# A shared expert's second product from 64 rows per half, and both second-pair gates ahead of the third layer's products, in a vision tower kernel

## The chip, the cores and the metric

The kernel runs on one core of a Trainium2 chip. The metric is the device time of one execution in microseconds (us), the median over a few executions; one further execution is recorded by the profiler.

## What is computed

Four images of 3 x 224 x 224 become 784 tokens of 64 numbers each (patches of 8 x 8, layer norm, two linear layers). Then come four residual blocks: a gated linear attention that here reduces to a product, a first layer of experts, a softmax attention with 8 heads, and a second layer of experts. The change is in the first layer of experts:

```python
# x: normalised tokens, 64 features; E = 4 experts, 2 chosen per token
h = relu(x @ sW1 + sb1)                 # shared path: 64 -> 64
h = relu(h @ sW2 + sb2)                 # 64 -> 128, the product that changes
shared = h @ sW3 + sb3                  # 128 -> 64
h = relu(x @ eW1[e] + eb1[e])           # each expert: 64 -> 128
h = relu(h @ eW2[e] + eb2[e])           # 128 -> 64
all_out[e] = h @ eW3[e] + eb3[e]        # 64 -> 64
out = shared + sum over the two best experts of topw * all_out[e]
```

## The kernel before

Features lie on the 128 partitions and tokens along them. The tokens of an image are split in two halves of 392; half 0 has its 64 features on partitions 0 to 63, half 1 on partitions 64 to 127. So one tile `[128, 392]` holds an image. Every engine has a program of its own, written out in order, and they meet through semaphores.

The first expert layer loops over the four images `b`. For each, TensorE issues in this order (the loop stands in the listing below):

- the experts' second layer (key "l2", pairs of experts p = 0, 1 and halves h = 0, 1): two products of 128 rows by 64 columns each, one for output partitions 0 to 63 and one for 64 to 127;
- the shared path's second product (key "s2", one for each half), line 853. Its weight `sw2` is `[128, 2, 128]`. The host fills rows 0 to 63 of part 0 and rows 64 to 127 of part 1 with `sW2` and leaves zeros in the other rows, so each product runs over all 128 rows of `s1`, though only 64 of them count;
- `gate_rows`: four transposes that turn the image's gate values into rows (key "wT");
- `first_layer(b + 1)`: the shared path's first product (key "s1"), and 8 outputs "l1" (4 experts, 2 halves) of two products each, in the format fp32r, for the next image;
- the third layer of image b: broadcasts of gates 0 and 1 (`broadcast_gate`, which spreads a gate's row over 128 partitions of bank 5 or 6), two products with `eb3r` (the output biases), two with `sw3` (the shared path), and then for m = 0 to 3 the broadcast of gate m + 2 if there is one, a wait until the m-th gated tile is ready, and the product `ew3` with it. Even m write partitions 0 to 63 of bank 7, odd m partitions 64 to 127.

A product of plain fp32 is two matmul instructions in the trace, one in fp32r is one. In the trace `s1` and `s2` are named `s`, `h1` and `h2` are `h`, the gate rows are `wT`, and all weights of the first table are `wa`. Nearly all products stand under line 679, the helper `mm`.

The outputs of the keys l2, s2, wT, s1 and l1 go round a ring of four PSUM banks (`bank_of`): an output may start once ScalarE has emptied the one four places before it. ScalarE (ACT) empties them one by one and in order with `hidden` (line 513), with bias and relu. VectorE (DVE) multiplies each `h2` tile by its broadcast gate in place (`times_gate`, line 1359): it waits for `wbc_full` and raises `wbc_done`. `broadcast_gate` for gate n waits until multiplication n - 2 is done, as the two banks 5 and 6 alternate. After the third layer VectorE adds bank 7 to `H` (line 1365), and ScalarE may write the next image's `h2`. After image 3 come the attention's layer norm (products with `H`, squares, variance, reciprocal root) and the attention.

Of the kernel before, what the change touches and what calls it, by code (L numbers as in the profile page):

```python
# [19 lines left out]
D = 64  # L20
# [14 lines left out]
E0, E1 = 4, 8  # L35
# [67 lines left out]
def build(nc, x, table_a, table_b, out):  # L103
    ctx = ExitStack()
    with ctx:
        def sem(name):
            return ctx.enter_context(nc.semaphore(name))

        def sb(stack, name, shape, dt=F32):
            return stack.enter_context(nc.sbuf_tensor(name, shape, dt))  # L110
# [19 lines left out]
        sel0r = sb(reg1, "sel0r", [96, E0 // 2, 2, 128], F32R)  # L130
# [22 lines left out]
        s1 = sb(reg1, "s1", [128, HALF])  # L153
        s2 = sb(reg1, "s2", [128, 2, HALF])
        gate0 = Gate(lambda n, shape, dt=F32: sb(reg1, n, shape, dt), E0)
        wT0 = sb(reg1, "wT0", [96, HALF], F32R)
# [43 lines left out]
        def bank(n, w=HALF):  # L200
            return P[:, n, 0:w]

        def A(name, rows=128):
            lo, hi = COLS_A[name]
            return wa[0:rows, lo:hi]
# [40 lines left out]
        hid_full, hid_done = sem("hid_full"), sem("hid_done")  # L246
# [430 lines left out]
        def _(pe):  # L677
            def mm(dst, lhsT, rhs, start=True, stop=True, **more):
                return nc.tensor.matmul(dst, lhsT, rhs, start=start, stop=stop, **more)  # L679
# [122 lines left out]
            def bank_of(key, first):  # L802

                k = HID[key]
                n, size = k % 4, 4
                if k - size >= first:
                    pe.wait_ge(hid_done, k - size + 1)
                elif k < size:
                    pe.wait_ge(h_ready, B)
                return n  # L810

            def gate_rows(n, wsp, b, full):
                for ct in range(NGT):
                    last = nc.tensor.transpose(P[0:96, n, ct * GT:(ct + 1) * GT], wsp[:, ct * B + b, :].bitcast(F32),  # L814
                                               Bt("ident", GT)[:, 0:GT])
                last.then_inc(full, 1)
# [3 lines left out]
            sw2 = A("sw2").rearrange("p (h n) -> p h n", h=2)  # L820

            def first_layer(b):
                mm(bank(bank_of(("s1", b), 0)), A("sw1"), xhat[:, b, :]).then_inc(hid_full, 1)
                pe.wait_ge(split0, 2 * b + 2)
                if b == 0:
                    pe.wait_ge(w0_split, 1)
                for e in range(E0):
                    for h in range(2):
                        n = bank_of(("l1", b, e, h), 0)
                        for part in range(2):  # L830
                            last = mm(bank(n), ew1r[:, part, e, :], xs0[:, b, h * HALF:(h + 1) * HALF], part == 0, part == 1)
                        last.then_inc(hid_full, 1)

            def broadcast_gate(sel, rows, n):

                if n >= 2:
                    pe.wait_ge(wbc_done, n - 1)
                mm(bank(WBC_BANKS[n % 2]), sel, rows).then_inc(wbc_full, 1)
# [4 lines left out]
            for b in range(B):  # L843
                for p in range(E0 // 2):
                    pe.wait_ge(hid_done, HID["l1", b, 2 * p + 1, 1] + 1)
                    for h in range(2):
                        n = bank_of(("l2", b, p, h), 0)
                        for e in range(2):
                            last = mm(P[e * D:(e + 1) * D, n, 0:HALF], ew2[:, 2 * p + e, :], h1[:, 2 * p + e, h, :])
                        last.then_inc(hid_full, 1)  # L850
                pe.wait_ge(hid_done, HID["s1", b] + 1)
                for h in range(2):
                    mm(bank(bank_of(("s2", b, h), 0)), sw2[:, h, :], s1[:, :]).then_inc(hid_full, 1)
                if b == 0:
                    pe.wait_ge(gates_ready, 1)
                gate_rows(bank_of(("wT", b), 0), gate0.wsp, b, hid_full)
                if b + 1 < B:
                    first_layer(b + 1)
                pe.wait_ge(hid_done, HID["wT", b] + 1)
                if b == 0:  # L860
                    pe.wait_ge(sel0_ready, 1)
                for m in range(2):
                    broadcast_gate(sel0r[:, 0, m, :], wT0[:, :], E0 * b + m)
                if b >= 1:
                    pe.wait_ge(h_ready, B + b)
                for part in range(2):
                    mm(bank(7), eb3r[:, part, :], wT0[:, :], part == 0, False, skip_group_check=True)
                for h in range(2):
                    mm(P[h * D:(h + 1) * D, 7, 0:HALF], A("sw3"), s2[:, h, :], False, False, skip_group_check=True)
                for m in range(E0):  # L870
                    if m + 2 < E0:
                        broadcast_gate(sel0r[:, 1, m, :], wT0[:, :], E0 * b + m + 2)
                    pe.wait_ge(wbc_done, E0 * b + m + 1)
                    h = m % 2
                    last = mm(P[h * D:(h + 1) * D, 7, 0:HALF], ew3[:, m // 2, :], h2[:, m // 2, h, :], False,
                              m // 2 == E0 // 2 - 1, skip_group_check=True)
                last.then_inc(moe_full, 1)
# [217 lines left out]
            for b in range(B):  # L1095
# [7 lines left out]
                for p in range(PAIRS):  # L1103
                    m = PAIRS * b + p
# [528 lines left out]
```

## Time and profile before

| what | value |
|---|---|
| median of three executions | 628.32 us |
| the three | 628.19, 628.32, 632.11 us |
| the profiled execution, its own time | 634.78 us |
| its span, first to last instruction | 633.0 us |
| mean granted TensorE clock | 0.979 of full |
| TensorE busy | 574.7 us, 91% |
| VectorE, ScalarE, GpSimd busy | 383.1, 335.3, 73.8 us |
| share of the chain that ended last | PE 87%, DVE 5%, ACT 4%, DMA 2% |

The profile is one execution. Its span is 1.8 us shorter than its own time, which has also what lies before the first and behind the last instruction. A matmul's time is its latency; consecutive ones overlap, so their cost is read from the distance of their starts.

### The profile page before, as it was taken

The numbers are of one execution on the slowest core, as the hardware profiler recorded it, in microseconds if no ns is written. First come the engines' busy times: TensorE is split into PE (matmuls) and PEld (weight loads), VectorE is DVE, ScalarE is ACT, GpSimd is POOL, SyncE is SP. The second block draws the span as 40 slices with busy tenths as digits, with TensorE's granted clock in tenths as the row PEclk, the third lists the DMA queues.
The fourth block names the chain that finished last, engine by engine and source line by source line (L and its number), as shares of the span: only waits on it lengthen the run. The fifth ranks groups of instructions, "written<-read, shape, count | busy, mean of one in ns | idle before, by whom it ended". The sixth has DMA issues, their size and how long they took to land.

```text
span 633.0 us, 10237 instructions
## 1 busy us (share of the span) xinstructions
PE 574.7 (91%) x3082; PEld 341.8 (54%) x3082; DVE 383.1 (61%) x896; ACT 335.3 (53%) x735; POOL 73.8 (12%) x88
## 2 busy tenths in 40 slices
PE   0597798999798999999999999999999999997992
PEld 0363344654446766757667566675666756452441
DVE  3847458123487776767767677676776765145561
ACT  0455857754654655646556465464664646525411
POOL 0000000000299001010010100101001010102000
PEclk9999899999897999999999999999999999997997
DMA  7500000000363233232332422323223220000024
GB/s 164 220 0 1 1 0 2 0 1 0 71 151 90 58 80 87 67 98 60 83 83 57 102 63 79 87 56 98 68 76 90 56 73 1 1 1 1 1 50 103
DMA packets 21986, 37.65 MB, mean 59 GB/s; under 512 B 5560, under 2 KB 15224, under 8 KB 21704
## 3 DMA queue, kind: packets, MB, share of 16 engines
q1 hardware_dynamic: 21816, 37.12, 22.9%
q10 hardware_dynamic: 144, 0.20, 0.2%
q8 instruction: 14, 0.23, 0.2%
q14 instruction: 12, 0.10, 0.0%
HBM read 6.07 MB, written 2.41 MB: 13 GB/s over the span
## 4 chain that ended last, share of the span: by engine, by line
PE 87%; DVE 5%; ACT 4%; DMA 2%; issue 1%; SPq 0%; DVEq 0%; ACTq 0%
PE P L679 83%; DMA X<-x 2%; PE P L695 2%; ACT L481 1%; DVE xhat L1204 1%; PE P L940 1%; ACT PT L590 1%; ACT g L622 1%; DVE xs L1273 1%; PE P L1079 0%; DVE mx L1378 0%; DVE gate_s L1261 0%; PE P L814 0%; DVE bst L1141 0%; PE P L910 0%
## 5 line engine op out<-in xcount | busy, mean ns | idle before, releaser
L1378 DVE TENSOR_REDUCE mx<-P 112x1 f32<-112x392 f32 x448 | 219.4, 558 | 97.2 <-PE P L679 92.5
L590 ACT ACTIVATE PT<-P 112x392 f32<-112x392 f32 x448 | 188.4, 494 | 27.3 <-PE P L679 26.1
L679 PE MATMUL P<-Ks,Qs 96*112 96x392 f32 x448 | 167.9, 379 | 1.0 <-DVE mx L1378 0.9
L679 PE MATMUL P<-Qs,Ks 98*112 98x392 f32 x448 | 155.5, 351 | 0.8 <-ACT PT L590 0.7
L679 PE MATMUL P<-PT,XVs 112*64 112x392 f32 x896 | 154.5, 496 | 0.0
L679 PEld LDWEIGHTS P<-PT,XVs 112*64 112x64 f32 x896 | 61.5, 137 | 79.5 <-issue 73.5
L679 PEld LDWEIGHTS P<-Ks,Qs 96*112 96x112 f32 x448 | 78.9, 178 | 42.6 <-issue 19.7
L598 ACT ACTIVATE CT<-P 128x392 f32<-128x392 f32 x32 | 15.9, 497 | 134.4 <-PE P L679 134.4
L679 PEld LDWEIGHTS P<-Qs,Ks 98*112 98x112 f32 x448 | 80.0, 179 | 6.2 <-ACT PT L590 3.7
L665 POOL TENSOR_TENSOR OUT<-OUT,part 120x448 f32<-120x448 f32 x27 | 30.7, 1138 | 274.2 <-DVE part L1405 274.2
L679 PE MATMUL P<-VBs,CT 128*112 128x130 f32 (+1 forms) x320 | 40.0, 261 | 0.6 <-ACT CT L598 0.6
L679 PEld LDWEIGHTS P<-VBs,CT 128*112 128x112 f32 (+1 forms) x320 | 35.3, 157 | 6.0 <-ACT CT L598 1.3
L653 POOL CAST QKH<-QKL 128x392 fp32r<-128x392 f32 x24 | 12.2, 507 | 168.7 <-ACT QKL L557 168.7
L513 ACT ACTIVATE h<-P,wa 128x392 f32<-128x392 f32 x48 | 24.9, 601 | 12.9 <-PE P L679 12.4
L1359 DVE TENSOR_TENSOR h<-P,h 128x392 f32<-128x392 f32 x16 | 8.7, 564 | 29.6 <-PE P L679 29.6
L679 PE MATMUL P<-xhat,wa 64*128 64x392 f32 (+2 forms) x88 | 24.7, 561 | 2.1 <-DVE xhat L1204 2.1
L695 PE MATMUL P<-wa,xn 112*96 112x112 f32 x56 | 12.1, 397 | 14.5 <-DVE xn L1154 14.5
L655 POOL TENSOR_TENSOR QKL<-QKL,QKH 128x392 fp32r<-128x392 f32 x24 | 24.4, 1017 | 1.9
L622 ACT ACTIVATE g<-P,wb 128x784 f32<-128x784 f32 x16 | 14.0, 911 | 14.5 <-PE P L679 14.4
L1508 DVE TENSOR_TENSOR g<-P,g 128x784 f32<-128x784 f32 x16 | 15.5, 974 | 9.1 <-PE P L679 9.1
L1405 DVE TENSOR_TENSOR part<-P,zi 120x448 f32<-120x448 f32 x32 | 20.0, 625 | 1.6
L1398 DVE RECIPROCAL zi<-P 120x7 f32<-120x7 f32 x32 | 6.4, 201 | 23.6 <-PE P L679 23.6
(180 smaller groups left out, 520.9 us busy)
## 6 DMA issues: line engine op xcount, KB each, us to landing
Qs<-QKH SPq DMA_DIRECT2D x64, 98.0 KB, 2.2
Ks<-QKH SPq DMA_DIRECT2D x64, 98.0 KB, 2.1
XVs<-XV SPq DMA_DIRECT2D x32, 196.0 KB, 2.5
Qs<-QKL SPq DMA_DIRECT2D x32, 98.0 KB, 2.1
Ks<-QKL SPq DMA_DIRECT2D x32, 98.0 KB, 2.1
X<-x SPq DMA_DIRECT2D x4, 588.0 KB
out<-OT SPq DMA_DIRECT2D x24, 98.0 KB
wa<-table_a SPq DMA_DIRECT2D x1, 2207.5 KB, 8.3
```

The lines of the kernel that those rows point to most:

```text
L513: nc.scalar.activation(dst, P[0:rows, k % 4, 0:width], func, **({} if bias is None else dict(bias=bias)))\
L590: nc.scalar.activation(PT[:, u, c * HALF:(c + 1) * HALF], P[0:T, SCORE_BANK + half_in_loop(s, u, c) % RING, 0:HALF], ACT.Exp, scale=float( ...
L598: nc.scalar.activation(CT[:, :], bank(6), ACT.Copy).then_inc(ctx_done, 1)
L622: nc.scalar.activation(g1[:, m // PAIRS, m % PAIRS, :, :], P[:, n:n + 2, 0:HALF], ACT.Gelu, bias=Bt("mb1")[:, m % PAIRS:m % PAIRS + 1]).th ...
L653: nc.gpsimd.tensor_copy(QKH[cols], QKL[cols].bitcast(F32)).then_inc(pool_hi, 1)
L655: nc.gpsimd.tensor_tensor(QKL[cols], QKL[cols].bitcast(F32), QKH[cols].bitcast(F32), ALU.subtract)\
L665: nc.gpsimd.tensor_tensor(OUT[:, b, :], OUT[:, b, :], part[:, h % HG % 3, :], ALU.add).then_inc(added, 1)
L679: return nc.tensor.matmul(dst, lhsT, rhs, start=start, stop=stop, **more)
L695: last = nc.tensor.transpose(P[0:KF, 2 * p + k, q * T:(q + 1) * T], xn[:, p, q, k * KF:(k + 1) * KF], A("ident", T)[:, 0:T])
L1378: nc.vector.tensor_reduce(mx[:, s % 2, c, t:t + 1], bank(n)[0:T, :], AX.X, ALU.max)\
L1405: nc.vector.tensor_tensor(part[:, s % 3, :].rearrange("p (t d) -> p t d", d=D), got[:, :, 0:D], zi[:, :].unsqueeze(2).broadcast_to([OROWS, ...
L1508: nc.vector.tensor_tensor(g1[:, b, p, :, :], P[:, n:n + 2, 0:HALF], g1[:, b, p, :, :], ALU.mult).then_inc(gate_used, 1)
```

## The change

The shared path's second product takes 64 rows of the weight and of `s1` instead of 128: rows 0 to 63 for half 0, rows 64 to 127 for half 1. The rows left out met only zeros. In the third layer the broadcasts of gates 2 and 3 both stand ahead of the four `ew3` products; before, gate 2 stood ahead of the first and gate 3 ahead of the second of them. The waits, the semaphores' counts, the banks and all other engines' programs stay as they are.

```diff
                 pe.wait_ge(hid_done, HID["s1", b] + 1)
                 for h in range(2):
-                    mm(bank(bank_of(("s2", b, h), 0)), sw2[:, h, :], s1[:, :]).then_inc(hid_full, 1)
+                    rows = slice(h * D, (h + 1) * D)
+                    mm(bank(bank_of(("s2", b, h), 0)), sw2[rows, h, :], s1[rows, :]).then_inc(hid_full, 1)
...
                     mm(P[h * D:(h + 1) * D, 7, 0:HALF], A("sw3"), s2[:, h, :], False, False, skip_group_check=True)
+                for m in range(2, E0):
+                    broadcast_gate(sel0r[:, 1, m - 2, :], wT0[:, :], E0 * b + m)
                 for m in range(E0):
-                    if m + 2 < E0:
-                        broadcast_gate(sel0r[:, 1, m, :], wT0[:, :], E0 * b + m + 2)
                     pe.wait_ge(wbc_done, E0 * b + m + 1)
                     h = m % 2
                     last = mm(P[h * D:(h + 1) * D, 7, 0:HALF], ew3[:, m // 2, :], h2[:, m // 2, h, :], False,
```

## Rows read from the trace of the kernel before

**Rows 1.** Chain that ended last, in time order, expert layer: start, length, what.

```profile
109.58 12.67 PE P L679 x56
...
148.29 0.59 ACT s L513
148.88 0.39 ACT wT L513
149.31 9.15 PE P L679 x34
```

**Rows 2.** Busy time in image 1's stretch: PE, PEld, DVE, ACT, POOL, clock, DMA.

```profile
122.08:135.09 13.01, 13.01 (x62) 7.52 (x60) 2.80 (x5) 8.31 (x17) 0.00 (x0) 1.00 0.00 1
```

**Rows 3.** Timeline of TensorE in image 0's third layer: start, length, what.

```profile
114.94 0.45 PE L679 MATMUL P<-wT,sel0r 96*128 96x392 f32 x1
...
115.31 0.54 PE L679 MATMUL P<-h,wa 128*64 128x392 f32 x1
...
115.69 0.49 PE L679 MATMUL P<-h,wa 128*64 128x392 f32 x1
...
116.12 0.45 PE L679 MATMUL P<-wT,sel0r 96*128 96x392 f32 x1
...
116.50 0.55 PE L679 MATMUL P<-h,wa 128*64 128x392 f32 x2
...
117.23 0.95 PE L679 MATMUL P<-h,wa 128*64 128x392 f32 x4
```

**Rows 4.** Timeline of VectorE in the same third layer: the four gate multiplications.

```profile
113.70 1.04 DVE L1359 TENSOR_TENSOR h<-P,h 128x392 f32<-128x392 f32 x2 [3.53 <-PE P L679]
115.42 0.57 DVE L1359 TENSOR_TENSOR h<-P,h 128x392 f32<-128x392 f32 x1 [0.68 <-PE P L679]
116.60 0.57 DVE L1359 TENSOR_TENSOR h<-P,h 128x392 f32<-128x392 f32 x1 [0.61 <-PE P L679]
```

**Rows 5.** Timeline of TensorE, image 3: the second of two adjoining broadcasts.

```profile
149.60 0.34 PE L679 MATMUL P<-wT,sel0r 96*128 96x392 f32 x1
```

**Rows 6.** Timeline of TensorE at image 1's second shared product and behind it.

```profile
120.66 0.60 PE L679 MATMUL P<-s,wa 128*128 128x392 f32 x1
...
121.75 0.49 PE L679 MATMUL P<-s,wa 128*128 128x392 f32 x1
...
122.08 0.25 PE L814 MATMUL P<-wb,gate_wsp 98*96 98x98 f32 x1
...
122.42 0.52 PE L679 MATMUL P<-xhat,wa 128*128 128x392 f32 x1
```

**Rows 7.** Timeline of ScalarE at the same place, one row for each emptied bank.

```profile
121.62 0.59 ACT L513 ACTIVATE s<-P,wa 128x392 f32<-128x392 f32 x1 [0.27 <-PE P L679]
...
122.28 0.59 ACT L513 ACTIVATE s<-P,wa 128x392 f32<-128x392 f32 x1
...
122.77 0.48 ACT L513 ACTIVATE wT<-P 96x392 fp32r<-96x392 f32 x1
...
123.31 0.59 ACT L513 ACTIVATE s<-P,wa 128x392 f32<-128x392 f32 x1
...
123.79 0.58 ACT L513 ACTIVATE h<-P,wa 128x392 f32<-128x392 f32 x1
```

**Rows 8.** Timeline of TensorE in the second expert layer: a 64-row product pair.

```profile
581.86 0.60 PE L679 MATMUL P<-xhat,wb 64*128 64x392 f32 x2 [0.36 <-ACT g L622]
...
582.30 0.50 PE L679 MATMUL P<-xhat,wb 64*128 64x392 f32 x2
```

**Rows 9.** Timeline of ScalarE, the eight l1 outputs of image 1.

```profile
110.79 3.92 ACT L513 ACTIVATE h<-P,wa 128x392 f32<-128x392 f32 x8
```

**Rows 10.** Timeline of TensorE: the gate turns of image 0.

```profile
109.04 0.54 PE L814 MATMUL P<-wb,gate_wsp 98*96 98x98 f32 x4 [1.19 <-DVE gate_wsp L1348]
```

**Rows 11.** Chain that ended last: the first two heads of the attention loop.

```profile
193.42 12.90 PE P L679 x56
...
206.42 11.26 PE P L679 x66
```

**Rows 12.** Stretches as in rows 2, at the start of that loop.

```profile
193.00:199.80 6.80, 6.72 (x22) 6.28 (x23) 6.02 (x12) 4.57 (x10) 6.48 (x9) 0.50 0.17 47
```

## The prediction

> **What bounds the kernel now.** I read the page's chain first: TensorE carries most of it. Then I read that chain in time order over the first expert layer. For images 0 to 2 it is one unbroken run of TensorE work per image, some 12.7 us long with the four gate turns between them [rows 1]; only at image 3 does it pass through ScalarE (the emptying of s, then of wT) before TensorE goes on [rows 1]. The table by stretches confirms it: in 13.01 us of one image TensorE is busy throughout, ScalarE 8.31, VectorE 2.80, at the full clock of 2.4 GHz [rows 2]. But "busy" counts latencies, and a run of waits shorter than a latency doesn't show. So the timelines decide, and the reader is to look at the distances between starts. They show two kinds of stretch. In the second and third layer TensorE sets the pace. In the first layer ScalarE does: it empties eight l1 outputs in 3.92 us, 0.47 to 0.49 us each [rows 9], and TensorE, with two products for each, is held back by the ring of four banks. A gain of TensorE's ahead of that stretch is therefore worth only what it also gives to ScalarE.
>
> **The gates ahead of the third layer's products.** Before, the order is: gate 2 at 114.94, product m=0 in two instructions at 115.31 and 115.69, gate 3 at 116.12, product m=1 together with m=2 at 116.50, and m=3 at 117.23 [rows 3]. Products 0 and 1 use different output partitions, and so could run side by side as m=1 and m=2 do (two starts within 0.01 us, 0.55 us for both), but gate 3 lies between them [rows 3]. After the change: gate 2 stays at 114.94. Gate 3 follows at the distance of two adjoining broadcasts behind a change of shape, 149.60 - 149.31 = 0.29 us [rows 1, 5], so at 115.22. Its bank must be free: the first two multiplications end at 113.70 + 1.04 = 114.74 [rows 4], so the wait that now stands ahead of m=0 has 0.48 us in hand. What is queued behind it are all four products and the next image's second layer. From gate 3 to m=0 the distance is 0.27 to 0.38 us (0.37 from gate to product now, and a broadcast behind another takes 0.34 where the first takes 0.45 [rows 3, 5]). I take 0.27, so m=0 and m=1 start at 115.49. Their second instructions come 0.38 later [rows 3], at 115.87, and m=2 could start some 0.33 behind these, at 116.20; it needs multiplication 2, which still ends at 115.99 [rows 4]. Product m=3 needs multiplication 3. That one's operand is now early, and VectorE does it right behind the one before: the first pair took 1.04 us for two where one takes 0.57 [rows 4], so it starts 0.48 after 115.42, at 115.90, and ends at 116.47. Now it ends at 117.17, and m=3 starts 0.06 later, at 117.23 [rows 3, 4]. So m=3 moves to about 116.51: **0.72 us** earlier. VectorE's chain, not TensorE's queue, sets this number: with 0.37 us instead of 0.27 ahead of m=0, m=2 would start at 116.30 and m=3 stays at 116.51. Everything behind m=3 (the next image's l2, or the norm of the attention after image 3) is TensorE work that is ready, and moves along. The other images have the same pattern, so four times 0.72 = **2.88 us**. Bounds for one image: at least 0.30, if m=0 and m=1 don't pair, so that m=1 starts with m=2 at 116.20 where they now start at 116.50 [rows 3]; at most 1.02, if m=3 could start with m=2 at 116.20, which rows 4 exclude.
>
> The expected reason for part of this is the change between 128x128 and 128x64 shapes: from a 64-column product's last instruction to a broadcast takes 0.42 us [rows 3], while two instructions of one shape stand 0.33 apart (121.75 to 122.08 [rows 6]). The Trainium skill, TensorEngine Tiling (Array Packing), "Key Properties", says that changing the tiling mode drains the engine; the reorder takes two such changes out for each image, and by that rule it speaks for this part. It speaks against the other one, below.
>
> **The second shared product from 64 rows.** Now its four instructions run one after another: 120.66 to 121.75, and the gate turns start at 122.08, 1.42 us behind the first [rows 6]. The trace has no 64-row pair at this place; the nearest is the second expert layer's first product, same shape, same two row halves, two banks: two starts within 0.01 us at 581.86, two more at 582.30, finished 0.94 us behind the start [rows 8]. The last of them starts 0.44 us in, and the next work is of another shape (98 rows), so 0.42 us is added where now 0.33 is enough [rows 3, 6]: gate turns at 0.86 us instead of 1.42. TensorE gains 0.56 us. By the skill's rule on changing modes this change adds a drain, here 0.09 us, and that is in the 0.86.
>
> ScalarE takes most of it back. Its first s starts at 121.62, 0.96 us behind the product's start [rows 6, 7]; the half-0 product of the pair ends at the same distance, 0.60 for the first instruction's row and 0.50 behind 0.44 for the second [rows 8], so that start doesn't move. The second s starts at 122.28 now, 0.66 later, since it waits for TensorE; now it can follow at ScalarE's own 0.47 [rows 9], at 122.09: 0.19 earlier. wT follows 0.49 behind it [rows 7], 122.58. Then s of the next image starts at 123.31, where 122.77 + 0.47 would have been possible: another 0.07 to be had, as its operand (the product at 122.42 [rows 6]) is 0.56 earlier. The first l1 output then starts at about 123.5 instead of 123.79 [rows 7]: **0.28 us**, bounds 0.19 and 0.33. From there ScalarE sets the pace, and TensorE leaves the first layer 0.28 us earlier, not 0.56. The Trainium skill says the same in TensorEngine Tiling (Array Packing), "PSUM Bottleneck": tiling speeds up TensorE and not the emptying of PSUM. Rows 7 and 9 agree.
>
> By image: image 0's shared product lies ahead of the gate turns that wait 1.19 us for VectorE's gates [rows 10], so it is hidden: 0. If that cover were gone it would be worth 0.28. Images 1 and 2 give 0.28 each. At image 3 no first layer follows, and the chain goes through both s, wT and then the broadcast [rows 1]: 0.19. Sum **0.75 us**.
>
> **The sum.** 2.88 + 0.75 = 3.63 us. The profiled execution of 634.78 us would be 631.15. Behind the layer everything follows in a chain from TensorE's products with H, so the shift carries through. The median shown, 628.32, lies 6.46 below the profiled time, and I take the same 3.6 off it: **624.7 us**, -0.58%. A measurement of this kernel can tell about 1% (6.3 us) from no change, so this counts as "within 1%".
>
> **Rivals.**
>
> 1. The clock shifts its steps. At 193.0 to 199.8 us TensorE runs at half clock, 1.2 GHz, after a stall ahead of the attention loop [rows 12]. The first head's 56 instructions took 12.90 us; at the next head's pace (66 in 11.26) it would be 9.55 [rows 11]. So 6.8 us at the low level cost 3.3 us. A stage that arrives 3.6 us earlier may lose half of that, or all, or gain as much again. That gives 621.4 to 628.0. For it: the three executions spread over 3.9 us with one program. Against it: the stall ahead of the loop isn't touched. Chance 0.14.
>
> 2. TensorE is the bound throughout and ScalarE's ring isn't: 2.88 + 3 x 0.56 = 4.6 us, 623.8. Against it speak rows 7 and 9. Chance 0.06.
>
> 3. The pairs don't form, or cost more than the nearest rows say: 4 x 0.30 = 1.2 us, 627.1. For it: m=0 and m=1 each wait for their own semaphore count; against it: m=1 and m=2 do too, and start together [rows 3]. Chance 0.10.
>
> 4. Slower: the earlier end of image 0's shared product lengthens TensorE's stall ahead of the gate turns from 1.19 [rows 10] to 1.75 us, and the clock falls to 1.2 GHz there, where it held 1.0 before. By rows 11 and 12 that costs 0.49 us for each microsecond at the low level. It decides against the change once the fall lasts over 3.63 / 0.49 = 7.4 us; a fall of 13.6 us costs 6.6 and gives 631.3. Of its chance of 0.07, some 0.03 end over 628.3.
>
> 5. Nothing changes that can be seen, since the stage isn't on the path: VectorE or a DMA later sets the start of the attention. Against it: the chain has TensorE without a break from 149.31 on [rows 1]. 628.3, chance 0.03.
>
> **How the numbers follow.** The forecast has 0.60; it and rivals 2 and 3 together 0.76, between 623.8 and 627.1. The range reaches over rival 1 down to 621.4, and up to the forecast with the spread of the executions on top, 624.7 + 3.9 = 628.6. Rival 4's long fall is left out. Faster by over 1% means below 622.0: only the far end of rival 1, with another small gain, 0.06. Slower by over 1% means above 634.6: 0.02. Within 1%: 0.92.
>
> **What the profile after would show.** Two adjoining broadcasts some 0.29 us apart behind the sw3 products, then m=0 and m=1 within 0.01 us; VectorE's third and fourth multiplication as one run of 1.04 us; m=3 about 1.57 us behind gate 2 instead of 2.29. The shared product's pair in 0.94 us, the two s of ScalarE 0.47 apart. The distance from image 1's to image 2's gate turns falls from 13.01 to 12.0 us, and the first broadcast of image 3, at 149.31 now [rows 1], comes 2.9 us earlier, at 146.4. From image 3's third layer on, the same distances as before. The forecast is wrong if m=3 waits for something other than VectorE, if TensorE's lead is lost in the first layer altogether, or if a stretch of low clock appears between 109 and 150 us.

## The result, and the profile after

| | kernel before | kernel after |
|---|---|---|
| median, 20 executions each | 632.66 us (628.19 to 635.74) | 628.86 us (626.51 to 629.51) |
| profiled execution, its own time | 634.78 us | 629.09 us |
| its span | 633.0 us | 627.3 us |

The ratio is 0.9936, with a 95% interval of 0.9919 to 0.9954: 0.64% faster, within 1%. (The two medians alone give 628.86 / 632.66 = 0.9940.) The medians differ by 3.80 us where 3.63 were forecast; the interval would allow anything from 2.9 to 5.1 us. The time itself, 628.86 us, lies 0.26 us above the range. The median of the kernel before had been 628.32 over three executions; over twenty it is 632.66.

The page of the kernel after begins so:

```profile
span 627.3 us, 10237 instructions
...
PE 570.2 (91%) x3082; PEld 339.8 (54%) x3082; DVE 382.5 (61%) x896; ACT 334.8 (53%) x735; POOL 73.8 (12%) x88
```

Next, the chain that ended last, in time order, as in [rows 1], and then stretches as in [rows 2].

```profile
108.22 0.89 PE P L814 x4
109.11 12.29 PE P L679 x55
121.40 0.47 PE P L814 x4
121.87 11.44 PE P L679 x55
...
145.27 1.05 ACT s L513 x2
146.32 0.38 ACT wT L513
...
146.75 3.48 PE P L679 x15
```

```profile
108.16:111.57 3.41, 3.35 (x10) 2.72 (x11) 1.13 (x3) 1.49 (x3) 0.00 (x0) 0.50 0.00 0
...
121.33:133.24 11.91, 11.91 (x63) 6.75 (x61) 2.70 (x5) 8.06 (x16) 0.00 (x0) 1.00 0.01 1
```

At the full clock an image takes 11.91 us instead of 13.01 [rows 2]. And in this execution the first image pays: from 108.16 to 111.57 us the granted clock is 0.50, that is 1.2 GHz. The gate turns at its beginning, as in [rows 10]:

```profile
108.22 0.89 PE L814 MATMUL P<-wb,gate_wsp 98*96 98x98 f32 x4 [1.44 <-DVE gate_wsp L1349]
```

They take 0.89 us against 0.54, behind a wait for VectorE's gates that the profile gives as 1.44 us instead of 1.19, as the shared product ahead of them ends earlier.

TensorE and VectorE in image 0's third layer, as in [rows 3] and [rows 4]:

```profile
115.45 0.45 PE L679 MATMUL P<-wT,sel0r 96*128 96x392 f32 x1
...
115.74 0.33 PE L679 MATMUL P<-wT,sel0r 96*128 96x392 f32 x1
...
116.00 0.55 PE L679 MATMUL P<-h,wa 128*64 128x392 f32 x2
...
117.03 0.54 PE L679 MATMUL P<-h,wa 128*64 128x392 f32 x2
```

```profile
114.22 1.04 DVE L1360 TENSOR_TENSOR h<-P,h 128x392 f32<-128x392 f32 x2 [4.87 <-PE P L679]
115.94 1.04 DVE L1360 TENSOR_TENSOR h<-P,h 128x392 f32<-128x392 f32 x2 [0.69 <-PE P L679]
```

Gate 3 follows gate 2 by 0.29 us. Products m=0 and m=1 start together at 116.00. Multiplications 2 and 3 are one run that ends at 116.98, and m=3 starts 0.05 behind it, at 117.03: 1.58 us behind gate 2, where it was 2.29 [rows 3]. Product m=2 stands 0.32 us ahead of m=3, so the two don't pair:

```profile
116.71 0.49 PE L679 MATMUL P<-h,wa 128*64 128x392 f32 x1
```

The second shared product of image 1 and ScalarE behind it, as in [rows 6] and [rows 7]:

```profile
120.47 0.60 PE L679 MATMUL P<-s,wa 64*128 64x392 f32 x2
...
120.90 0.50 PE L679 MATMUL P<-s,wa 64*128 64x392 f32 x2
...
121.33 0.29 PE L814 MATMUL P<-wb,gate_wsp 98*96 98x98 f32 x1
```

```profile
121.43 0.59 ACT L513 ACTIVATE s<-P,wa 128x392 f32<-128x392 f32 x1 [0.27 <-PE P L679]
...
121.91 0.58 ACT L513 ACTIVATE s<-P,wa 128x392 f32<-128x392 f32 x1
...
122.38 0.49 ACT L513 ACTIVATE wT<-P 96x392 fp32r<-96x392 f32 x1
...
122.76 0.58 ACT L513 ACTIVATE s<-P,wa 128x392 f32<-128x392 f32 x1
...
123.23 0.59 ACT L513 ACTIVATE h<-P,wa 128x392 f32<-128x392 f32 x1
```

The pair forms as in the second expert layer [rows 8], and the gate turns start 0.86 us behind it instead of 1.42. ScalarE's first s still starts 0.96 us behind the product. Its first l1 output starts 2.76 us behind it, instead of 3.13 (120.66 to 123.79, [rows 6, 7]): a gain of 0.37 out of TensorE's 0.56.

### The profile page after: what moved, and what is told of

Its sections match the earlier page's. It is cut to its first block, busy times and chain, and to the rows that moved or that the text cites. A ratio compares the mean times of both kernels' runs of the same rounds, so it can differ in the third digit from the quotient of the medians.

```text
span 627.3 us, 10237 instructions
## 1 busy us (share of the span) xinstructions
PE 570.2 (91%) x3082; PEld 339.8 (54%) x3082; DVE 382.5 (61%) x896; ACT 334.8 (53%) x735; POOL 73.8 (12%) x88
## 4 chain that ended last, share of the span: by engine, by line
PE 86%; DVE 4%; ACT 4%; DMA 3%; issue 1%; SPq 1%; DVEq 0%; ACTq 0%
PE P L679 82%; DMA X<-x 2%; PE P L695 2%; ACT L481 1%; DVE xhat L1205 1%; PE P L941 1%; ACT PT L590 1%; ACT g L622 1%; DVE xs L1274 1%; PE P L1080 0%; PE P L814 0%; SPq L370 0%; DVE gate_s L1262 0%; DMA Ks<-QKH 0%; DVE bst L1142 0%
```

## The experiments

Two lengths are read from each trace as differences of starts. The **distance** goes from image 1's gate turns to image 2's. The **layer** goes from image 0's gate turns to the first product with H of the attention's norm (109.04 to 154.12 us before, 108.22 to 150.85 after). These are the first products with H in the kernel before, in the kernel after, and in the kernel after profiled once more (after_again):

```profile
154.12 0.60 PE L679 MATMUL P<-H,wb 128*128 128x392 f32 x1
...
150.85 0.60 PE L679 MATMUL P<-H,wb 128*128 128x392 f32 x1
...
150.78 0.60 PE L679 MATMUL P<-H,wb 128*128 128x392 f32 x1
```

The gate turns of image 0 in after_again, from the chain:

```profile
109.48 0.54 PE P L814 x4
```

The low clock column says whether the profiled execution had a stretch at 0.50 in the layer's first 4 us. Each ratio is to executions of the kernel before that were taken beside that kernel; their medians were 632.52 us (35 executions; gates_only, s2_only, after_hold, before_hold), 632.88 (13; ring3, dve_s2, both, after_warm) and 632.16 (21; the other four).

| kernel | distance | layer | low clock | median (executions) | ratio to before |
|---|---|---|---|---|---|
| before | 13.01 | 45.08 | no | 632.66 (20) | 1 |
| after | 11.91 | 42.63 | yes | 628.86 (20) | 0.9936 (0.9919 to 0.9954) |
| after_again | 11.92 | 41.30 | no | 629.26 (12) | 0.9950 (0.9922 to 0.9978) |
| gates_only | 12.30 | 42.25 | no | 629.01 (12) | 0.9941 (0.9916 to 0.9966) |
| s2_only | 12.63 | 44.12 | no | 631.57 (12) | 0.9984 (0.9958 to 1.0010) |
| after_hold | 11.93 | 41.32 | no | 628.33 (12) | 0.9935 (0.9908 to 0.9961) |
| before_hold | 13.01 | 45.07 | no | 633.58 (12) | 1.0009 (0.9977 to 1.0041) |
| ring3 | 11.42 | 40.63 | yes | 626.56 (6) | 0.9901 (0.9864 to 0.9938) |
| dve_s2 | 11.77 | 40.53 | no | 626.80 (8) | 0.9902 (0.9868 to 0.9935) |
| both | 11.29 | 38.57 | no | 627.69 (6) | 0.9891 (0.9842 to 0.9941) |
| after_warm | 11.91 | 43.72 | yes | 625.72 (6) | 0.9890 (0.9854 to 0.9926) |
| before_warm | 13.01 | 45.08 | no | 628.24 (10) | 0.9933 (0.9904 to 0.9963) |
| both_warm | 11.28 | 39.78 | yes | 622.38 (6) | 0.9841 (0.9798 to 0.9884) |
| both_warm_hold | 11.27 | 38.55 | no | 622.10 (6) | 0.9830 (0.9793 to 0.9868) |

The layer's length repeats within 0.02 us where the clock does (41.30 and 41.32; 45.07, 45.08 and 45.08; 38.57 and 38.55), while medians of six to twenty executions of kernels with the same layer differ by up to a microsecond (before and before_hold, 632.66 and 633.58). So the verdicts on single parts go by the layer.

**One part alone: the gates.**

```diff
                 for h in range(2):
-                    rows = slice(h * D, (h + 1) * D)
-                    mm(bank(bank_of(("s2", b, h), 0)), sw2[rows, h, :], s1[rows, :]).then_inc(hid_full, 1)
+                    mm(bank(bank_of(("s2", b, h), 0)), sw2[:, h, :], s1[:, :]).then_inc(hid_full, 1)
```

> Only the broadcasts of gates 2 and 3 stand ahead of the four ew3 products; the shared path's second product keeps its 128 rows. Theory (VectorE's multiplication 3 sets m=3): 0.72 us for each of four images, 2.9 us in all, ratio 0.9954; m=3 starts 1.57 us behind gate 2, and the distance from image 1's to image 2's shared product is 13.0 - 0.72 = 12.3 us. Rival (the pair of m=0 and m=1 is worth nothing, only the order counts): 0.30 for each, ratio 0.998. Rival (all of the gain comes from the shared product): 13.0 us, ratio 1.0.

Stretches of its trace, from image 1's gate turns to image 2's:

```profile
116.99:129.29 12.30, 12.30 (x62) 7.22 (x61) 2.70 (x5) 8.32 (x17) 0.00 (x0) 1.00 0.01 1
```

13.01 - 12.30 = 0.71 us for an image, and 45.08 - 42.25 = 2.83 us for four. In image 0 m=3 starts 1.58 us behind gate 2, as in the kernel after. The theory stands, and both rivals fall.

**The other part alone: 64 rows.** The kernel before with only the first hunk of the change.

> Only the shared path's second product is taken from 64 rows; the third layer keeps its order. Theory (ScalarE sets the pace behind it): the distance from image 1's to image 2's shared product falls from 13.0 by 0.28 to 0.38 us, in all 0.75 to 1.0 us, ratio 0.9985. Rival (TensorE sets the pace): 0.56 for each of three images, distance 12.45, 1.7 us, ratio 0.9973.

```profile
121.04:133.67 12.63, 12.63 (x63) 6.97 (x61) 2.80 (x5) 8.07 (x16) 0.00 (x0) 1.00 0.01 1
```

0.38 us for an image and 45.08 - 44.12 = 0.96 us in the layer: inside what the theory gave, far from the rival's 0.56. The two parts add up: 2.83 + 0.96 = 3.79 us, and 45.08 - 41.30 = 3.78 with both. By the medians alone this part can't be told from nothing (interval up to 1.001).

**Who takes back the rest: ScalarE.** VectorE empties the shared outputs of images 1 to 3. The waits on `hid_done` count only what ScalarE empties; the banks of these outputs and the `sw3` products wait for `s2_done`.

```diff
+                for h in range(2 if b else 0):
+                    k = HID["s2", b, h]
+                    vector.wait_ge(hid_full, k + 1)
+                    nc.vector.tensor_scalar(s2[:, h, :], bank(k % 4), col("sb2"), 0.0, ALU.add, ALU.max).then_inc(s2_done, 1)
                 for e in range(E0):
                     times_gate(E0 * b + e, h2[:, e // 2, e % 2, :])
...
-                    for h in range(2):
-                        hidden(("s2", c, h), s2[:, h, :], ACT.Relu, col("sb2"))
+                    if c == 0:
+                        for h in range(2):
+                            hidden(("s2", c, h), s2[:, h, :], ACT.Relu, col("sb2"))
```

> The changed kernel, with the two shared outputs of images 1 to 3 emptied by VectorE (add, then max with 0) instead of ScalarE. If ScalarE is what takes back part of the 64-row product's gain, its s of the next image starts as soon as TensorE has it, 0.2 us earlier for images 1 and 2, and wT of image 3 some 0.5 us earlier: about 0.9 us in all, distance 11.7 us. Rival (TensorE is the bound there already): distance 11.91 as in the changed kernel, same median.

ScalarE in its trace, at image 1 (the shared product starts at 119.34) and at image 3 (142.88):

```profile
120.78 0.49 ACT L518 ACTIVATE wT<-P 96x392 fp32r<-96x392 f32 x1 [0.74 <-PE P L822]
121.47 0.59 ACT L518 ACTIVATE s<-P,wa 128x392 f32<-128x392 f32 x1 [0.19 <-PE P L685]
...
144.31 0.49 ACT L518 ACTIVATE wT<-P 96x392 fp32r<-96x392 f32 x1 [0.74 <-PE P L822]
```

ScalarE now waits for TensorE, 0.74 us ahead of wT and 0.19 ahead of s, where in the kernel after it had one wait of 0.27 us. The layer is 0.77 us shorter (41.30 to 40.53), the distance 0.15. So ScalarE was the bound there. The 0.9 us expected was 0.13 too much: no more than 0.15 an image was to be had, since s of the next image now waits for TensorE again. TensorE's product for it starts 1.24 us behind the shared product (120.58 - 119.34) where it was 1.76 [rows 6], so TensorE had gained 0.52 us at that point, of which 0.37 came through in the kernel after and 0.37 + 0.15 = 0.52 do here. What follows, ScalarE's pace through the eight l1 outputs, this edit doesn't touch.

**The third layer with three gate banks.**

```diff
-        WBC_BANKS = (5, 6)
+        WBC_BANKS = (4, 5, 6)
...
-                if n >= 2:
-                    pe.wait_ge(wbc_done, n - 1)
-                mm(bank(WBC_BANKS[n % 2]), sel, rows).then_inc(wbc_full, 1)
+                if n >= 3:
+                    pe.wait_ge(wbc_done, n - 2)
+                mm(bank(WBC_BANKS[n % 3]), sel, rows).then_inc(wbc_full, 1)
...
-                for m in range(2):
-                    broadcast_gate(sel0r[:, 0, m, :], wT0[:, :], E0 * b + m)
+                for m in range(3):
+                    broadcast_gate(sel0r[:, m // 2, m % 2, :], wT0[:, :], E0 * b + m)
...
+                broadcast_gate(sel0r[:, 1, 1, :], wT0[:, :], E0 * b + 3)
                 for h in range(2):
                     mm(P[h * D:(h + 1) * D, 7, 0:HALF], A("sw3"), s2[:, h, :], False, False, skip_group_check=True)
-                for m in range(2, E0):
-                    broadcast_gate(sel0r[:, 1, m - 2, :], wT0[:, :], E0 * b + m)
...
-                nc.vector.tensor_tensor(buf, bank(WBC_BANKS[n % 2]), buf, ALU.mult).then_inc(wbc_done, 1)
+                nc.vector.tensor_tensor(buf, bank(WBC_BANKS[n % 3]), buf, ALU.mult).then_inc(wbc_done, 1)
```

> The changed kernel with three banks (4, 5, 6) for the broadcast gates instead of two. Gates 0, 1 and 2 are broadcast at once, gate 3 behind the eb3r products, so that all four stand in one shape ahead of the sw3 and ew3 products. If VectorE's late multiplications 2 and 3 are what sets m=3 in the changed kernel, they now follow the first two without a gap, m=3 starts with m=2, and one more change of shape goes: 0.7 us for each image. Distance from image 1's to image 2's shared product 11.9 - 0.7 = 11.2 us, median 2.8 us below the changed kernel's, ratio to before about 0.989 to 0.990. Rival (TensorE's own products set it): distance stays at 11.7 to 11.9.

VectorE and TensorE in its trace, image 1:

```profile
126.01 1.98 DVE L1359 TENSOR_TENSOR h<-P,h 128x392 f32<-128x392 f32 x4 [7.56 <-PE P L679]
```

```profile
126.63 0.44 PE L679 MATMUL P<-wT,sel0r 96*128 96x392 f32 x1
127.00 0.88 PE L679 MATMUL P<-s,wa 128*64 128x392 f32 x4
127.71 1.49 PE L679 MATMUL P<-h,wa 128*64 128x392 f32 x8
```

The four multiplications are one run, and behind gate 3 all products stand in one shape, without a gap, m=2 and m=3 side by side: TensorE is the bound here. The distance falls by 0.50, less than the 0.7 expected, since gate 3 has to wait for multiplication 0 (it starts 0.05 us behind it), and costs a gap of its own. In the layer it is 2.00 us for four images (42.63 to 40.63, both with the low clock). The edit does two things at once: m=3 no longer waits for VectorE (the 0.32 us by which it stood behind m=2), and the change from the products' shape to the broadcasts' and back is gone. This run doesn't part them, so how much of the 0.50 is VectorE's isn't shown.

**The stall ahead of the gate turns.** Two useless products (one in the kernel before) fill it.

```diff
                 if b == 0:
+                    for _ in range(2):
+                        mm(bank(7), A("sw1"), xhat[:, 0, :])
                     pe.wait_ge(gates_ready, 1)
```

> The changed kernel, with two extra products of 128x128x392 whose result is never used, behind image 0's shared product, so that TensorE works 1.3 of the 1.75 us in which it would stand still ahead of image 0's gate turns. If that stall is what lowers the clock at 108 to 112 us, the stretch is gone, the distance from image 0's gate turns to the first broadcast of image 3 is 40.27 - 2.9 = 37.4 us at the most, instead of the 38.5 in the profile of the changed kernel, and the median is up to 1.1 us lower. Rival (the clock falls there by chance, whatever TensorE does in the stall): the median stays within 0.3 us of the changed kernel's, 628.9.

> The kernel before with one such extra product (0.66 of 1.19 us of stall filled): the control. If the low stretch at the gate turns comes only with the change's longer stall, this kernel is the same as before within 0.3 us. If the kernel before had it too in a share of its executions, it is faster by up to 1 us, and the spread of its times (628.2 to 635.7) narrows.

The filled kernel's layer is 41.32 us, with no low stretch, and from image 0's gate turns to image 3's first broadcast it is 37.21 us (109.38 to 146.59), within what was expected. (The stall to be filled was 1.44 us, as the profile above shows, and not the 1.75 of the expectation; with two products nothing is left of it.) But the unfilled kernel, profiled again, has no low stretch either, and 41.30. So one profile of each can't say that the filling held the clock; the medians (628.33 against 628.86 and 629.26) lean that way and don't decide, and the control shows nothing. Over all profiles: of eight with the 64-row pair and an unfilled stall, four had the low stretch (after, ring3, after_warm, both_warm) and four not; of the three without the pair and unfilled, none; of the three that are filled, none. That the longer stall (1.44 us instead of 1.19) makes the fall more frequent is likely and not shown. What it costs when it comes is shown: a stretch of 3.41 us costs 42.63 - 41.30 = 1.33 us in the kernel after. In after_warm, whose layer is the same, the stretch is twice as long, 0.83 us of it ahead of the gate turns, and the layer is 43.72 - 41.30 = 2.42 us longer:

```profile
105.19:112.02 6.83, 6.00 (x19) 5.37 (x20) 1.82 (x5) 4.20 (x8) 0.00 (x0) 0.50 0.00 0
```

**Both edits in one kernel.** The edits of ring3 and dve_s2 together.

> Three gate banks and VectorE's emptying together. If the two bounds are independent the gains add: distance 11.0 us, 3.7 us below the changed kernel, ratio to before about 0.988. If VectorE now gets in the way of itself (the shared outputs stand ahead of the gate multiplications in its queue), it is no faster than the three banks alone.

The layer is 38.57 us, 2.73 less than after_again's, with a distance of 11.29: near the sum of 2.00 and 0.77, but 1.0 us short of the 3.7 expected, as the two parts had been, 0.8 and 0.1 us, by themselves. The median of six, 627.69, doesn't show it: two executions lie at 621.68 and 622.07, four between 627.60 and 629.26. The last table of the next part shows where the profiled one, 628.55, lost it.

**The spread between executions.** Two useless products behind the variance products of four norms, where TensorE waits 2.52 us for ScalarE (with them 1.00 us is left):

```diff
                 last.then_inc(var_full, 1)
+                if S in (TOK2, POOL3, ATT, MOE1):
+                    for _ in range(2):
+                        mm(bank(6), Bt("center"), square_buf(S)[:, 0, :])
```

> The changed kernel with two extra products of 128x128x392, result never used, behind the variance products of four of the six norms, where TensorE stands still for 2.5 us. If the spread between executions (626.5 to 629.5 for the changed kernel, 628.2 to 635.7 for the kernel before) comes from the clock falling behind these stalls, the stretches of low clock at 67 to 74 and 159 to 163 us are gone or shorter, the spread narrows towards the low end, and the median is 1 to 2.5 us lower. Rival (the falls come from other stalls, or the extra work delays the chain): the same median or up to 1 us more.

> The changed kernel once more, as the yardstick for the three beside it on the same chip: ratio to before 0.994, median 628 to 629.5, distance from image 1's to image 2's shared product 11.9 us.

> The kernel before with the same two extra products behind four norms' variance products as in the run with the changed kernel (625.7 there against 628.9 without). If the spread and the higher median of the kernel before come from clock falls behind those stalls, it gains at least as much: median 629 to 630, ratio about 0.995 to 0.996, spread under 4 us. If the gain with the changed kernel was chance of the sample, ratio 1.0. The distance between shared products stays 13.0 us.

The kernel after with them (after_warm) has a median of 625.72 us, 3.1 below 628.86, more than the 1 to 2.5 expected; its executions spread over 3.5 us, where without them it was 3.0, so the spread didn't narrow. The kernel before with them gains 0.67%, 628.24 against 632.16 us, by work that it doesn't need, with every distance in the expert layer unchanged, and its spread is 3.8 us against 7.0. The difference of the two profiled executions, 634.78 and 625.96 us, isn't all owed to the extra products; part of it lies ahead of the first of them. The same 5 us of the tokenizer's end, first in the profile of the kernel before, then in that of gates_only, whose programs are equal up to there:

```profile
43.00:48.00 5.00, 5.00 (x23) 1.88 (x21) 0.00 (x0) 3.11 (x5) 0.00 (x0) 1.00 0.00 0
```

```profile
43.00:48.00 5.00, 4.95 (x33) 2.88 (x34) 1.44 (x3) 4.18 (x7) 0.00 (x0) 1.00 0.00 0
```

And the four products of 64x512 there, in the same two traces:

```profile
46.53 1.97 PE L679 MATMUL P<-wa 64*64 64x512 f32 x4
```

```profile
45.42 1.08 PE L679 MATMUL P<-wa 64*64 64x512 f32 x4
```

1.97 against 1.08 us, and the starts of the first and the second pair of instructions 0.90 against 0.47 apart: by these distances the first is at the low level, though the clock column says 1.00 for both. From the first pixel statistics to the first variance product it is 33.78 us in twelve of the fourteen profiles and 31.15 in two (gates_only and before_warm), so this alone is worth 2.6 us, and no edit of mine reaches it.

Behind it, the extra products do act. This is in how many profiles the granted clock is 0.50 in a stretch at these places:

| place | ten profiles without them | four with them |
|---|---|---|
| behind the second norm (64 to 75 us) | 10 | 2 |
| behind the attention's norm (153 to 166 us) | 8 | 0 |
| ahead of the attention loop (180 to 200 us), no extra products there | 10 | 4 |
| behind the second expert layer's norm (565 to 579 us) | 8 | 0 |

(gates_only and before_warm, whose tokenizer's end is fast, have one more, at 55 to 58 us.) The last of these places in after_again and in dve_s2, one of the two that have no low stretch there without extra products:

```profile
568.81:572.22 3.41, 3.18 (x10) 1.05 (x12) 1.80 (x5) 0.00 (x0) 3.16 (x4) 0.50 0.01 2
```

```profile
564.00:575.00 11.00, 8.54 (x44) 3.15 (x44) 5.87 (x13) 6.81 (x8) 3.93 (x4) 1.00 0.00 0
```

The times go with it. From the last context product of the attention to the end it is 75.66 to 75.67 us in all six profiles without a low stretch there (the four with the extra products, ring3 and dve_s2), and 76.48 to 77.83 in the eight that have one. From the first product behind the attention's norm (`P<-rs,spread`, 160.97 us in the kernel before) to the first context product it is 37.55 to 38.35 with them, against 38.08 to 39.89. From the first variance product to image 0's gate turns it is 55.59 to 56.14 us in the three with them that left the tokenizer at the low level, against 57.79 to 58.91 in nine without; where the tokenizer's end was fast, it is 56.67 with them (before_warm) and 56.68 without (gates_only). So the extra products take low clock away behind the last two norms in which they stand. How the gain in the median of either kernel divides between this and the tokenizer's end, one profile of each can't say.

The same cut for four profiled executions, in us:

| stretch | before | after | after_again | both |
|---|---|---|---|---|
| to the first pixel statistics | 17.31 | 16.55 | 16.83 | 16.74 |
| to the first variance product | 33.78 | 33.77 | 33.78 | 33.77 |
| to image 0's gate turns | 57.95 | 57.90 | 58.88 | 58.87 |
| the layer | 45.08 | 42.63 | 41.30 | 38.57 |
| to the first product behind the attention's norm | 6.85 | 6.85 | 6.86 | 6.85 |
| to the first context product | 39.62 | 38.61 | 38.50 | 39.89 |
| to the last context product | 354.56 | 354.47 | 354.61 | 354.45 |
| to the end | 77.83 | 76.50 | 76.48 | 77.61 |
| span | 632.98 | 627.29 | 627.23 | 626.75 |

Two profiled executions differ by much more than the change. The spans of before and after_again are 5.75 us apart, of which the layer has 3.78. And the kernel with both further edits, whose layer is 2.73 us shorter than after_again's, loses 1.39 + 1.13 us of it behind the layer, in stretches where the programs are equal. Whether it does so by chance, or because its attention and its end come earlier and meet the clock's steps elsewhere, no run here decides.

**All together.**

> Three gate banks, VectorE's emptying of the shared outputs and the extra products in the norms together. If the gains in the expert layer (3.3 us by the distances of the run with both) and of the norms (some 3 us) add, the median is 622 to 623, ratio 0.983 to 0.985. If a clock fall at the gate turns takes them back, 624 to 625.5.

> The same with two further extra products ahead of image 0's gate turns. If the fall at 105 to 112 us in the trace of the changed kernel with warmed norms comes from the stall there, it is gone and this is 1 to 2 us faster than without. Rival (the extra products delay the gate turns as much as they save, as the gate turns of the first run of this kind lay 1.0 us later relative to the pixels): the same within 0.5 us.

An image in the last kernel's trace:

```profile
117.78:129.05 11.27, 11.27 (x62) 6.49 (x60) 3.77 (x7) 7.25 (x14) 0.00 (x0) 1.00 0.01 1
```

622.38 and 622.10 us: 1.6 and 1.7% faster than the kernel before, and better than the change alone by far more than its interval. The two can't be told from each other by the medians. In the profiles the unfilled one has the low stretch at the gate turns (0.51 granted from 105.69 to 109.10) and the filled one hasn't; the layer is 39.78 against 38.55 us.

```profile
105.69:109.10 3.41, 3.01 (x9) 2.38 (x10) 1.43 (x4) 1.15 (x3) 0.00 (x0) 0.51 0.00 0
```

## Why the prediction was right in its change and wrong in its time

**What held.** The order of the third layer: predicted 0.72 us an image and 2.88 in all, measured 0.71 and 2.83. VectorE's multiplication 3 sets m=3, as said: 0.05 us lie between its end and that product. The distance from gate 2 to m=3 was to be 1.57 us and is 1.58. The 64-row pair forms as the second expert layer's does, and TensorE gains the 0.56 us forecast. The part of it that counts was mis-sized: 0.28 us an image and 0.75 in all were forecast, 0.37 and 0.96 measured. The term was the step from wT to s: I let ScalarE take its 0.47 us there; behind wT it goes on after 0.38 (122.38 to 122.76). That it had waited there for TensorE's operand was noted, and its size was put at 0.07 where it was 0.16. So the whole came to 0.37, beyond the upper bound of 0.33 too. The right step could have been read from the kernel before: ScalarE's copies without a bias mostly go on after 0.38 to 0.39 us (the last section has the rows), and wT is one. The sum, 3.63, was 3.78 in the layer by the traces at equal clock (before and after_again). That the medians differ by 3.80, so close to it, is partly luck: the two profiled spans lie 5.7 us apart, of which the layer has 2.45, and after_again's median, 629.26, lies 2.90 below that of the kernel before beside it.

**What failed.** The step "The median shown, 628.32, lies 6.46 below the profiled time, and I take the same 3.6 off it". The number was one of three, and the three didn't agree: 628.19, 628.32, 632.11, and a profiled fourth of 634.78. In the twenty executions that the result rests on, three lie at 628.2 to 628.3, the other seventeen from 630.66 to 635.74. So two of the three were of the rare kind, by chance, and the two that I set aside, 632.11 and 634.78, of the usual. The change taken off 632.66 gives 629.03, against 628.86 measured. Taken off the profiled time, 631.15, it would have been 2.3 too high. The range had room only for "the spread of the executions on top", 3.9 us; a start 4.3 us too low used it up. The runs show where such a spread is from: stretches of low clock that executions meet or don't in parts where their programs are equal, 2.6 us at the tokenizer's end, about 2 at the end of the kernel, and 1.8 between the attention's norm and its loop. The gap between the kernel before's two groups (628.32 to 630.66) has about the size of the first, but no execution of the lower group was profiled, so which stretch makes it isn't shown.

**The rivals.** Rival 1 was right in kind, and was tied to the wrong thing. I let the clock move only with the shift of 3.6 us; it moves without any, as the two profiles of the kernel after show (1.33 us in the layer). Whether a shift moves it as well stays open. Rival 2 (TensorE the bound throughout) fell with s2_only. Rival 3 (no pairs) fell with the trace. Rival 4's mechanism came in part: a stretch of 3.41 us at the low level at the place named, in the profile after, worth 1.33 us instead of the 1.7 that its 0.49 us for each microsecond gives. So the last of the signs that the prediction gave of being wrong did appear, in one of the kernel's two profiles. The longest at this place, 6.83 us in after_warm, is short of the 7.4 us from which it would have decided. The stall ahead of it grew to 1.44 us and not to 1.75: the pair doesn't form at image 0, and the last of the shared product's instructions starts only 0.25 us nearer to the first (0.82 instead of 1.07). Rival 5 fell: from the first product with H to the first behind the attention's norm it is 6.85 to 6.86 us in all fourteen profiles, so nothing else sets the start of what follows.

## What to carry to other kernels

Before a time is forecast, look whether the few executions shown agree with each other and with the profiled one; where they fall into groups, forecast a change, and let the range span the groups. When an engine that feeds another becomes faster, follow the consumer's own pace from its first late start: here two thirds of a 0.56 us gain came through. A useless product in a stall can pay where the stall lets the clock fall, and the traces, stage by stage, tell its worth better than a median of a few executions does.

## What the runs showed of the hardware that was not expected

Useless work made the kernel faster: two extra products in each of four norms' stalls took 0.67% off the kernel before (0.9904 to 0.9963). Behind two of these stalls of 2.52 us the granted clock fell to 0.50 in eight of ten profiles, and in none of four with the stall cut to 1.00 us. The clock column can say 1.00 at the start of a trace where the products' distances are those of the low level: 1.97 us against 1.08 for the same four.

And ScalarE's pace isn't one number: from PSUM with a bias operand it goes on 0.47 us after the start of the one before, without one mostly after 0.38 to 0.39 (14 of the 15 steps between copies to `QKL`; one took 0.49). That wT has 96 rows isn't the reason. The copies ahead of the attention loop have 128 rows and no bias, and eight of them take 3.30 us, where eight of the same shape with a bias take 3.92 [rows 9]:

```profile
168.61 3.30 ACT L557 ACTIVATE QKL<-P 128x392 f32<-128x392 f32 x8
```

The norms' squares come from one line of the kernel before in both kinds, with the bias `biasc` and without, 586 and 497 ns each:

```profile
L477 ACT ACTIVATE sq<-P,biasc 128x392 f32<-128x392 f32 x12 | 6.8, 586 | 7.1 <-PE P L679 6.9
...
L477 ACT ACTIVATE sq<-P 128x392 f32<-128x392 f32 x4 | 2.0, 497 | 5.0 <-PE P L679 5.0
```
